# Pairing the 48-row half of an expert's down product in the two halves of TensorE's array

## The reference

```python
xn = layernorm(x)
out = x + attn(xn, Wq, bq, Wk, bk, Wv, bv) + ffn(xn, ...)
# attn: 8 heads of 32 channels, a decaying linear attention (retention), in chunks
# ffn: mixture of experts
scores = softmax(xn @ gate_w.T)                  # 64 experts
topk_w, topk_ids = top_k(scores, 6)              # normalised to sum 1
gu = einsum('th,efh->tef', xn, w_gate_up)        # per expert 2*176 columns
act = silu(gu[..., :176]) * gu[..., 176:] * comb[:, :, None]
routed = einsum('tef,ehf->th', act, w_down)      # 176 -> 256
shared = (silu(sg) * su) @ ws_down.T             # one shared expert of width 352
```

## Time and profile before

| | before |
|---|---|
| median of 3 runs | 279.9 us (279.69 to 281.68) |
| the profiled execution's own time | 279.9 us |
| its span | 278.1 us |
| PE busy | 266.8 us (96%) |
| POOL busy | 186.8 us (67%) |
| DVE, ACT busy | 167.9 us (60%), 161.4 us (58%) |
| mean granted TensorE clock | 0.991 |

### The profile page before, as it was taken

The page is one execution under the profiler, slowest core; times in us unless marked ns, Lnnn a source line. Parts: engine busy times, 40 slices in busy tenths (PEclk is TensorE's granted clock), DMA queues, the critical chain, the costliest instruction groups (busy, mean ns, idle before and its releaser), DMA issues.

```text
span 278.1 us, 6626 instructions
## 1 busy us (share of the span) xinstructions
PE 266.8 (96%) x1778; PEld 192.2 (69%) x1778; DVE 167.9 (60%) x485; ACT 161.4 (58%) x412; POOL 186.8 (67%) x175
## 2 busy tenths in 40 slices
PE   8899989699999999999999999999999999979995
PEld 6675656477777777877777777777677754568873
DVE  3959965489766566575665665756656444144452
ACT  1357963676777766767767767676776533301111
POOL 1194855557877777777777777777774542999920
PEclk9999999999999999999999999999999999979998
DMA  7997922779798888898999998889751017974111
GB/s 209 308 376 269 303 73 66 261 257 309 262 308 273 298 267 270 289 290 280 306 291 283 290 305 266 292 258 317 222 155 60 27 48 259 392 271 157 41 37 60
DMA packets 28391, 64.70 MB, mean 233 GB/s; under 512 B 6180, under 2 KB 14092, under 8 KB 28368
## 3 DMA queue, kind: packets, MB, share of 16 engines
q1 hardware_dynamic: 20704, 48.02, 52.5%
q0 software_dynamic: 7664, 16.41, 18.6%
HBM read 58.67 MB, written 11.01 MB: 251 GB/s over the span
## 4 chain that ended last, share of the span: by engine, by line
PE 86%; DVE 8%; DMA 2%; ACT 1%; issue 1%; SPq 0%; DVEq 0%
PE ps_four L1172 27%; PE ps L1201 14%; PE ps L1200 10%; PE ps_four L1158 5%; PE ps L1182 5%; PE ps_four L1263 5%; PE ps L1301 4%; PE ps_four L1080 2%; PE ps_four L1283 2%; PE ps_four L1113 2%; DMA x_slab<-in_x 2%; DVE one_hots L781 2%; PE ps L1310 1%; PE ps L1071 1%; PE ps_four L1125 1%; DVE one_hots L770 1%
## 5 line engine op out<-in xcount | busy, mean ns | idle before, releaser
L465 POOL DMA_INDIRECT digits<-table,gcol x65 | 68.4, 1052 | 27.6 <-issue 12.8
L471 POOL DMA_INDIRECT picks<-y,scol x65 | 66.7, 1026 | 25.3 <-issue 18.0
L1172 PE MATMUL ps_four<-w_split,xT_both 128*128 128x352 f32 x390 | 79.8, 339 | 1.4 <-ACT xT_both L580 1.4
L1172 PEld LDWEIGHTS ps_four<-w_split,xT_both 128*128 128x128 f32 x390 | 60.6, 188 | 23.1 <-issue 22.6
L826 DVE SCALAR_TENSOR_TENSOR act<-ps_four,digits,sg 128x176 f32<-128x176 f32 x64 | 25.6, 400 | 54.7 <-ACT sg L586 48.2
L834 DVE TENSOR_TENSOR w_split<-w_ring,w_split 128x704 fp32r<-128x704 f32 x65 | 57.3, 882 | 0.6 <-issue 0.4
L574 ACT CAST w_split<-w_ring 128x704 fp32r<-128x704 f32 x65 | 51.0, 784 | 0.0
L599 ACT COPY y<-ps 128x256 f32<-128x256 f32 x65 | 24.3, 375 | 42.4 <-PE ps L1201 40.3
L1201 PE MATMUL ps<-w_slab,aT 48*128 48x256 f32 x130 | 45.2, 428 | 0.0
L1200 PE MATMUL ps<-w_ring,aT 128*128 128x256 f32 x130 | 39.0, 382 | 0.0
L1201 PEld LDWEIGHTS ps<-w_slab,aT 48*128 48x128 f32 x130 | 19.1, 184 | 21.5 <-issue 21.5
(11 more groups left out here) (176 smaller groups left out, 339.9 us busy)
## 6 DMA issues: line engine op xcount, KB each, us to landing
w_ring<-in_w SPq DMA_DIRECT2D x65, 480.0 KB, 3.8
w_slab<-in_w SPq DMA_DIRECT2D x65, 48.0 KB, 4.8
picked_rows<-picks SPq DMA_DIRECT2D x4, 768.0 KB, 4.5
back_b<-picks SPq DMA_DIRECT2D x4, 768.0 KB, 5.6
digits<-table,gcol POOLq DMA_INDIRECT x65, 4.7
picks<-y,scol POOLq DMA_INDIRECT x65
x_slab<-in_x SPq DMA_DIRECT2D x4, 256.0 KB, 3.6
table<-tab_slab POOLq DMA_DIRECT2D x1, 1024.0 KB, 10.1
```

The source lines that it names most:

```text
L465: pool.indirect_dma_start(out=rows[:, r, :], out_offset=None, in_=table, in_offset=bass.IndirectOffsetOnAxis(ap=gcol[:, r:r + 1], axis=0), ...
L471: pool.indirect_dma_start(out=picks, out_offset=bass.IndirectOffsetOnAxis(ap=scol[:, k % 8:k % 8 + 1], axis=0), in_=y[:, k % 4, :], in_off ...
L1172: ins = mm(ps[2 + k % 2][:, 0:2 * F], rr(a[:, k % 2, h * P:(h + 1) * P]), rr(b[:, k % (2 if b is w_lo else 4), h * 2 * F:(h + 1) * 2 * F]) ...
```

## The change

The 48-row part (`down_rest`) leaves `down` and runs for two tiles at once, at the end of every even step: first the even tile (t-2), whose rest rows stand in partitions 0 to 47, then the odd one (t-1), whose rest rows now stand in partitions 64 to 111. For that the weights `w2` of odd slots are loaded to partitions 64 to 111, and `trans_act` of an odd tile turns columns 64 to 191 instead of 128 to 255. Since an even tile's first part now waits for its second part over two steps, `aT` has four buffers; since the results of two tiles come together, `evac_y` runs for two tiles at the head of every odd step of ACT, and there are eight buffers of y, four of them in `tab_slab`. The computation is the same.

```diff
+REST_AT = (0, 64)
+REST_COLS = (P, 64)
+Y_RING = 8
...
-        aT = sb("aT", [P, 2, 2 * P])
+        aT = sb("aT", [P, 4, 2 * P])
...
+        y_slots = [y[:, n, :] for n in range(4)] + [tab_slab[:, n * H:(n + 1) * H] for n in range(Y_RING - 4)]
...
+            def w2_rows(slot):
+                return slice(REST_AT[slot % 2], REST_AT[slot % 2] + F2)
...
-                sp.dma_start(w2_sb[:, slot, :], w2[e, :, :]).then_inc(w_in[slot], 16)
+                sp.dma_start(w2_sb[w2_rows(slot), slot, :], w2[e, :, :]).then_inc(w_in[slot], 16)
...
             def evac_aT(t, k):
                 act_e.wait_ge(aT_ps, t + 1)
-                if not (isinstance(t, int) and t < 2):
-                    act_e.wait_ge(y_ps, t - 1)
+                if not (isinstance(t, int) and t < 4):
+                    act_e.wait_ge(y_ps, t - 3)
...
             def expert_act(i, k, ahead=3):
                 t = i * RING + k
-                if not (isinstance(t, int) and t < 2):
-                    evac_y(t - 2, k - 2, isinstance(t, int) and t < 6)
+                if k % 2 == 1 and not (isinstance(t, int) and t < 3):
+                    for back_by in (3, 2):
+                        evac_y(t - back_by, k - back_by, isinstance(t, int) and t - back_by < Y_RING)
...
-                for h in range(2):
+                for h, at in enumerate((0, REST_COLS[k % 2])):
                     ins = nc.tensor.transpose(ps[4 + k % 2][:, h * P:(h + 1) * P],
-                                              act[:, k % 2, h * P:(h + 1) * P], ident)
+                                              act[:, k % 2, at:at + P], ident)
...
+            def down_rest(k, slot):
+                rest = slice(REST_AT[k % 2], REST_AT[k % 2] + F2)
+                return mm(ps[6 + k % 2][:, 0:H], aT[rest, k % 4, P:2 * P], w2_sb[rest, slot, :], start=False, stop=True)
...
-                mm(ps[6 + k % 2][:, 0:H], aT[:, k % 2, 0:P], w1_sb[:, slot, 4 * F:W1C], start=True, stop=False)
-                mm(ps[6 + k % 2][:, 0:H], aT[0:F2, k % 2, P:2 * P], w2_sb[0:F2, slot, :],
-                   start=False, stop=True).then_inc(y_ps, 1)
+                mm(ps[6 + k % 2][:, 0:H], aT[:, k % 4, 0:P], w1_sb[:, slot, 4 * F:W1C], start=True, stop=False)
...
                 if not first:
                     down(t - 1, k - 1, (k - 1) % RING, listed)
+                if k % 2 == 0 and not first:
+                    for kk in (k - 2, k - 1):
+                        down_rest(kk, kk % RING).then_inc(y_ps, 1)
```

More of the change, by code:

```diff
@@ L190, in build @@
         w2_slab = slab("w2_slab", RING * H)
-        w2_sb = view(w2_slab, 0, RING, H)[0:F2]
+        w2_sb = view(w2_slab, 0, RING, H)
         ks = view(w2_slab, 0, NC, H)
@@ L270, in build @@
         y_ps, y_sb = sem("y_ps"), sem("y_sb")
-        picks_out = [sem(f"picks_out{k}") for k in range(4)]
+        picks_out = [sem(f"picks_out{k}") for k in range(Y_RING)]
         act_zero, silu_zero = sem("act_zero"), sem("silu_zero")
@@ L305, in build @@
         LISTED = (8,)
-        STORES = [len(range(k, TILES, 4)) for k in range(4)]
+        STORES = [len(range(k, TILES, Y_RING)) for k in range(Y_RING)]
         def all_picks_out(engine, n_ov):
             engine.wait_ge(picks_out[0], n_ov * 16 + 16 * STORES[0])
-            for k in range(1, 4):
+            for k in range(1, Y_RING):
                 engine.wait_ge(picks_out[k], 16 * STORES[k])
@@ L472, in scatter @@
                     out=picks, out_offset=bass.IndirectOffsetOnAxis(ap=scol[:, k % 8:k % 8 + 1], axis=0),
-                    in_=y[:, k % 4, :], in_offset=None,
-                    bounds_check=T * TOPK - 1, oob_is_err=False).then_inc(picks_out[k % 4], 16)
+                    in_=y_slots[k % Y_RING], in_offset=None,
+                    bounds_check=T * TOPK - 1, oob_is_err=False).then_inc(picks_out[k % Y_RING], 16)
             pool.wait_ge(gcol_ready, 1)
@@ L589, in evac_aT @@
                 act_e.wait_ge(aT_ps, t + 1)
-                if not (isinstance(t, int) and t < 2):
-                    act_e.wait_ge(y_ps, t - 1)
-                nc.scalar.copy(aT[:, k % 2, :], ps[4 + k % 2][:, 0:2 * P]).then_inc(aT_sb, 1)
+                if not (isinstance(t, int) and t < 4):
+                    act_e.wait_ge(y_ps, t - 3)
+                nc.scalar.copy(aT[:, k % 4, :], ps[4 + k % 2][:, 0:2 * P]).then_inc(aT_sb, 1)
             def evac_y(t, k, first):
@@ L596, in evac_y @@
                 if not first:
-                    act_e.wait_ge(picks_out[k % 4], (t - k) * 4 + 16 * (k // 4))
-                nc.scalar.copy(y[:, k % 4, :], ps[6 + k % 2][:, 0:H]).then_inc(y_sb, 1)
+                    act_e.wait_ge(picks_out[k % Y_RING], (t - k) * (16 // Y_RING) + 16 * (k // Y_RING))
+                nc.scalar.copy(y_slots[k % Y_RING], ps[6 + k % 2][:, 0:H]).then_inc(y_sb, 1)
             def number_tokens(c):
@@ L643, in expert_act @@
                 evac_aT(t, k)
-            for k in range(6):
+            for k in range(Y_RING + 2):
                 expert_act(0, k)
             with act_e.Fori(0, E // RING - 1) as i:
-                for k in range(6, RING + 6):
+                for k in range(Y_RING + 2, RING + Y_RING + 2):
                     expert_act(i, k)
-            for k in range(6, RING + EXTRA):
+            for k in range(Y_RING + 2, RING + EXTRA):
                 expert_act(E // RING - 1, k, ahead=min(3, RING + EXTRA - 1 - k))
-            for k in range(RING + EXTRA - 2, RING + EXTRA):
+            for k in range(RING + EXTRA - 3, RING + EXTRA):
                 evac_y(E - RING + k, k, False)
@@ L926, in expert_dve @@
                 if not first:
-                    dve.wait_ge(picks_out[k % 4], (t - k) * 4 + 16 * (k // 4 - 1))
+                    dve.wait_ge(picks_out[k % 8], (t - k) * 2 + 16 * (k // 8))
                 if last and k >= RING:
@@ L1232, in _ @@
             down(TILES - 1, RING + EXTRA - 1, EXTRA - 1)
+            down_rest(RING + EXTRA - 1, EXTRA - 1).then_inc(y_ps, 1)
             pe.wait_ge(ov_ready, 1)
@@ L1246, in _ @@
                     down(t, 0, 0)
+                    down_rest(0, 0).then_inc(y_ps, 1)
             pe.wait_ge(y_sb, n_ov + TILES)
```

6 lines of the change are left out of this document (3 added, 3 removed).

## The result

The changed kernel takes 290.4 us (median of 6 runs, 286.97 to 293.82) against 281.6 us for the kernel before, run beside it (6 runs, 279.69 to 284.33). The ratio of the undisturbed runs is 1.024, 95% interval [1.019, 1.029]: slower by 2.4%, some 6.7 us; clear of no change, with a lower end just under 2%. So the sign is wrong, and the time lies outside the range. The one of the changed kernel's runs with a mean granted clock of 0.986 took 287.2 us, and the kernel before, run beside the experiments, 280.6 to 281.7 at that mean clock: at the same clock the loss is there too, about 2%. The profiled execution of the changed kernel took 293.8 us, the longest of its six.

A forecast was written before the change was run, and what follows sets the result against it. PE and POOL were both taken as limits at 2.65 us a tile, POOL setting the loop's end: 212.9 + 1.0 + 2.4 + 6.95 + 1.3 = 224.6 against 225.54, so 278.9 us from 279.9; range 276.4 to 280.8.

The forecast's parts named there:

- PE's own saving: PE in the expert loop: paired 48-row parts save 0.83 us a pair; after ACT and DVE delays, 0.3 us a tile.
- I take the pair as one rest part: PE's array: two 48-row parts overlap fully and cost as one, 0.63 us in the chain.
- a pair of steps takes about 4.7 us: PE's loop: two tiles take about 4.7 us against 5.30, or about 5.0 with nothing overlapped.
- POOL as the second bound: Expert loop: POOL needs a gather and a store per tile, 2.65 us, PE's own period, so no slack.
- Store 0 at 61.7: POOL's first store: starts at 61.7 instead of 60.22, as tile 0's y waits for tile 1's; 1.4 us late.
- With y always there, stores 55 to 58 and gather 64 follow at 1.32: End of POOL's loop: from store 54 at 206.34, gather 64 comes at 212.9, against 215.56, before POOL's start shift of 1.0.
- the crossover: Expert loop, after 17 to 50 of 65 tiles: PE, 5 to 8 us ahead, then waits for each gather at POOL's pace.
- The five long operations: POOL between 64.36 and 77.30: five operations took 1.24 to 1.70 us instead of 1.02, 2.5 us too long; cause left open.
- the slower rival: POOL in the loop: fuller DMA holds operations 2.5 us more, on top of a 1.4 late start; 283.1 us, chance 0.08.
- The landing: Tile 64's gather, from its start until its rows can be turned: 2.4 us, between 2.0 and 3.0.
- The clock in the tail: Tile 64's way to its y: a PE hole of 3 to 5 us drops the clock, costing 1.3 us, between 0 and 1.9.
- The new order at the end: Last tiles on PE: pair 62 and 63, then 64 alone, costs 0 to 0.1 us.

The follow-up runs named there:

- a9: Changed kernel with w_low in two halves, gather 64 before store 56, and both 48-row parts in the lower half of the array: 1.000 against the kernel before.
- a4: Changed kernel with only the gather of tile 64 moved ahead, before store 56, w_low whole: 285.0 us, 1.011 against the kernel before.
- b3: Kernel before with the gather of tile 64 put before store 56: 280.6 us, ratio 1.000.
- a8: Changed kernel with gather 64 before store 56 and w_low in two halves, the second behind x_low: 281.7 us, 1.001 against the kernel before.

## Why the prediction was wrong, by its own steps

- **PE's own saving: the overlap right, the step too short.** The pair takes 0.63 to 0.68 us in the chain, 1.06 in one half. "I take the pair as one rest part" held. The rule that the prediction weighed against it, strict order in the Trainium skill's "TensorE: Matmul & The Clock Gate", Part 3, would have cost some 0.2 us a pair; the trace shows at most 0.05. But "a pair of steps takes about 4.7 us" measured 4.93, from 89.67 to 94.60 in the chain after:

```profile
89.67 1.18 PE ps_four L1181 x6
...
91.72 1.38 PE ps_four L1181 x6
...
94.60 1.15 PE ps_four L1181 x6
```

  The second product was put at 0.95 us and took 1.38, its third matmul waiting for `x_low` (0.43 us where 0.15 to 0.3 were allowed). So PE gained 0.19 us a tile and not 0.3, and with both parts in one half nothing at all (5.29 in a9, where "about 5.0" was forecast). It isn't what made the forecast fail, since POOL set the time.
- **POOL as the second bound: right**, and so was the first sign of it: PE waits for gathers from the middle of the loop on, 3.90 us before the last L1167.
- **Store 0 at 61.7: right.** It started at 66.04, less the 4.3 us of the late start 61.7.
- **"With y always there, stores 55 to 58 and gather 64 follow at 1.32", and from the crossover on "at POOL's 2.65 us a tile": this is the step that failed.** Gather 64 was put at 212.9 + 1.0 = 213.9; it started at 228.68 - 4.3 = 224.4, 10.5 us later. The 1.32 was read from a loop in which POOL met `w_low` almost never, and taken for a property of the operation. It is 1.02 + 0.30 only in that rhythm. Once PE runs ahead and has to wait for POOL, the starts of `w_low`, which wait for PE, and of the stores move against each other (this is my reading of the two timelines; that they collide is counted), and over a quarter of the 130 operations (35) were held, 34 of them begun under a `w_low`, for 10.2 us more in all than before.
- **The five long operations** were the clue. I left it open whether they "were held by something that doesn't move with them", and the slower rival laid them to DMA being fuller. All five began under a `w_low` (the first at 64.36, under one from 64.03 to 64.92: 0.43 us over, 0.43 by the rule). They were the price of a rhythm that the kernel before passed through for 14 us (64 to 78) and then left; the change keeps coming back to it. The rival had the right engine, the right symptom and the right side, with a wrong cause, 2.5 us where it was 10.2, and a chance of 0.08.
- **The landing: right,** 2.43 us against 2.4.
- **The clock in the tail: right as a mechanism, too small.** "I take 1.3, between 0 and 1.9" measured 2.3 us (9.87 against a4's 7.58 at full clock): the half clock lasted 6.8 us and not 3.4. The new order at the end, "worth 0 to 0.1", cost another 0.6 (7.58 against 6.97). Runs a4 and b3 put the hole and the clock at about 1.3% of the changed kernel.
- **The range** was made of the bounds of landing, clock and start. It had no term for POOL's pace, because I never asked what sets the 1.02 us.

Open: why the piece of `w_low` behind the first sometimes keeps POOL out and sometimes not; and whether an order of DVE's work can be found in which POOL never starts under `w_low`. Putting `w_low` before or behind DVE's other steps, apart from a8's split, wasn't tried.

## What to carry to other kernels

When two engines have the same period, the one with idle time only outside the loop is a second bound: shortening the first one's step gains little by itself and can let them collide. Before counting on a second engine's pace, line up each operation that is longer than its fellows in the old trace with what the other engines do at that moment; here five such rows told the price of a loss that came 35 times. Where POOL issues indirect DMAs beside DVE, try DVE's long SBUF-to-SBUF instructions in shorter pieces (here two halves did it and four quarters did no better), and look whether POOL starts just ahead of them or just behind.

## What the runs showed of the hardware that I had not expected

- An indirect DMA of 128 rows that starts on POOL under a DVE instruction of 128x704 from SBUF ends 0.89 us after that instruction does; one that starts 0.18 us ahead of it takes its 1.02 us, and DVE's instruction its usual 0.88. Both a subtraction of two tensors (0.88 us) and a `tensor_scalar` of one (0.52 us) hold it so. The `tensor_scalar` also held the 16 that had begun 0.44 to 0.59 us ahead of it, until 0.12 us after its end; the subtraction none of 16 such.
- Cutting the DVE instruction in two lowers the held time from 13.2 to 5.3 us; in four it is no better (5.1 us with the other order at the end, against 4.6 with two), with nine operations held past the end of the piece that they began under.
- Leaving out the 48-row product, which took the busiest engine (96%) from 266.8 to 244.8 us of busy time, made the kernel 2.3% slower.
- Two 48-row matmuls of float32 in the two halves of the array take 0.63 to 0.68 us together in the chain, 1.06 in the same half.
- A hole in which PE was busy for 1.31 of 4.2 us was followed by 6.8 us of granted clock 0.50, and the way of the last tile took 2.3 us more than at full clock.
